# ScalarE's order in the attention phase of a fused attention, experts, scan and ternary FFN kernel

## What is computed

```
x = x + conv0(layernorm_c(x))   # e1, e2 = relu(w1 xn), relu(w2 xn); softmax(e1^T e2) mixes xn; + relu(w3 xn)
t = t + moe(layernorm(t))       # 16 experts, top 4 of each token, and a shared expert
x = x + scan(layernorm_c(x))    # rows top to bottom and back: relu(Wm carry + b) + row
t = t + ternary_ffn(layernorm(t))  # weights w / mean|w| rounded to -1, 0, 1; silu(gate) * up; down
```

## Time and profile before

| what | value |
|---|---|
| median of 3 runs | 1029.52 us |
| lowest to highest | 1026.97 to 1030.14 us |
| profiled execution, its own time | 1030.67 us |
| its span | 1029.0 us |
| busy share PE / DVE / ACT / POOL | 91% / 63% / 52% / 14% |

### The profile page before, as it was taken

One profiled execution on the slowest core, in us unless ns is written; L12 is line 12 of the kernel. 1 busy time (PEld: TensorE's weight loads), 2 busy tenths in 40 slices (PEclk: granted clock), 3 DMA queues, 4 the chain that ended last, 5 costly groups with the idle time before them and its releaser, 6 DMA issues. The chain is left out here.

```text
span 1029.0 us, 21177 instructions
## 1 busy us (share of the span) xinstructions
PE 939.9 (91%) x7748; PEld 617.7 (60%) x7749; DVE 651.2 (63%) x1272; ACT 538.3 (52%) x857; POOL 139.3 (14%) x165
## 2 busy tenths in 40 slices
PE   5988997899999999999999999999999949975796
PEld 4444544567766766766676677667754438862453
DVE  5366788456665645665656665665656776667773
ACT  3665596256564544564546655555653212234674
POOL 0000001102210110210120112012106800002000
PEclk9988998999999999999999999999999979997998
DMA  8770544776786576675568856867886510000001
GB/s 285 250 245 1 207 160 152 222 224 212 269 262 205 195 232 196 225 270 189 193 233 258 256 203 228 258 194 234 266 253 196 169 36 1 1 0 1 1 21 62
DMA packets 164882, 181.76 MB, mean 177 GB/s; under 512 B 54609, under 2 KB 132433, under 8 KB 164850
## 3 DMA queue, kind: packets, MB, share of 16 engines
q1 hardware_dynamic: 152338, 147.35, 44.4%
q0 software_dynamic: 9808, 32.12, 9.7%
q10 hardware_dynamic: 2704, 1.87, 0.6%
HBM read 155.09 MB, written 14.68 MB: 165 GB/s over the span
## 5 line engine op out<-in xcount | busy, mean ns | idle before, releaser
L1090 DVE SCALAR_TENSOR_TENSOR w_lo<-raw_first,w_hi 128x1024 f16<-128x1024 f32 x144 | 172.6, 1223 | 76.7 <-ACT w_hi L581 76.7
L848 PE MATMUL pa<-x,w_hi 128*128 128x256 f16 (+2 forms) x576 | 171.2, 297 | 8.3 <-DVE between L1097 5.7
L850 PE MATMUL pa<-x,w_lo 128*128 128x256 f16 (+2 forms) x576 | 171.1, 297 | 0.0
L849 PE MATMUL pa<-x,w_hi 128*128 128x256 f16 (+2 forms) x576 | 171.0, 297 | 0.0
L848 PE MATMUL pb<-x,w_hi 128*128 128x256 f16 (+2 forms) x576 | 170.9, 297 | 0.0
L849 PE MATMUL pb<-x,w_hi 128*128 128x256 f16 (+2 forms) x576 | 170.9, 297 | 0.0
L850 PE MATMUL pb<-x,w_lo 128*128 128x256 f16 (+2 forms) x576 | 170.8, 296 | 0.0
L581 ACT ACTIVATE w_hi<-raw_first 128x1024 f16<-128x1024 f32 x144 | 147.8, 1049 | 2.2 <-DMA raw_first<-in_gate_up 2.2
L589 ACT CAST early<-between 128x320 f16<-128x320 f32 (+1 forms) x144 | 68.4, 475 | 151.1 <-DVE between L1097 151.1
L1090 DVE SCALAR_TENSOR_TENSOR w_lo<-raw_last,w_hi 128x1024 f16<-128x1024 f32 x72 | 88.2, 1224 | 76.1 <-ACT w_hi L581 76.1
L1102 DVE TENSOR_TENSOR early<-between,early 128x320 f16<-128x320 f32 (+1 forms) x144 | 74.0, 514 | 74.2 <-ACT early L589 74.1
(11 more groups left out here) (273 smaller groups left out, 1623.0 us busy)
## 6 DMA issues: line engine op xcount, KB each, us to landing
raw_first<-in_gate_up SPq DMA_DIRECT2D x96, 512.0 KB, 4.7
raw_last<-in_gate_up SPq DMA_DIRECT2D x32, 512.0 KB, 3.9
raw_first<-in_down SPq DMA_DIRECT2D x32, 512.0 KB, 4.6
raw_last<-in_down SPq DMA_DIRECT2D x32, 512.0 KB, 3.6
chunks<-in_f SPq DMA_DIRECT2D x16, 704.0 KB, 5.7
slot_y<-chunks POOLq DMA_DIRECT2D x16, 512.0 KB, 3.2
chunks<-in_f SPq DMA_DIRECT2D x6, 768.0 KB, 4.8
raw_first<-in_sgate SPq DMA_DIRECT2D x6, 512.0 KB, 6.3
```

The source lines that it names most:

```text
L848: T.matmul(out, hi_a, hi_b, start=first, stop=False, **flags)
L849: T.matmul(out, hi_a, lo_b, start=False, stop=False, **flags)
L850: return T.matmul(out, lo_a, hi_b, start=False, stop=last, **flags)
L1090: V.scalar_tensor_tensor(w_lo[:, j % RING, c], raw[j % RING][:, c], W_SCALE, w_hi[:, j % RING, c], ALU.mult, ALU.subtract).then_inc(split_ ...
```

## The change

On ACT: behind `exp(3)`, `exp(4)`, `exp(5)` and `exp(6)` the next `relu` and `turned_copy` stand at once, ahead of the `hi`, `sum_abs` and `make_ternary` calls that preceded them. The scan's weight copy goes from ahead of `exp(3)` to behind `sum_abs(5)`. At `exp(7)`, `turned_copy(6)` changes places with `make_ternary(1)`. On DVE: the scan weights' four instructions go from behind `row_max(3)` to behind `row_max(5)` and `lo(0, 0, 1)`, and the two instructions of the ternary scale go from behind `add_attention(4)` to directly behind `row_max(6)`. PE, POOL and SP keep their lists. No instruction is added or removed.

```diff
 # ACT
             turned_copy(1)
+
+            exp(3)
+            relu(2)
+            turned_copy(2)
+            hi(0, 0, 0)
+            sum_abs(5)
             act.wait_ge(conv_in, 32)
             S.copy(conv_hi[:, :, :], conv).then_inc(conv_hi_ready, 1)
             S.copy(bias_hi[:, :], bias).then_inc(conv_hi_ready, 1)
-
-            exp(3)
-            hi(0, 0, 0)
-            sum_abs(5)
             sum_abs(6)
-            relu(2)
-            turned_copy(2)
             sum_abs(7)
 
             exp(4)
+            turned_copy(3)
             hi(0, 0, 1)
             sum_abs(8)
             sum_abs(9)
-            turned_copy(3)
             sum_abs(10)
 
             exp(5)
+            relu(3)
+            turned_copy(4)
             sum_abs(11)
             hi(0, 1, 0)
-            relu(3)
-            turned_copy(4)
             hi(0, 1, 1)
 
             exp(6)
-            make_ternary(0)
             turned_copy(5)
             hi(0, 2, 0)
+            make_ternary(0)
 
             exp(7)
             zn_copy(0)
             x_high(0)
+            turned_copy(6)
             make_ternary(1)
-            turned_copy(6)
             zn_copy(1)
             x_high(1)
 # DVE: these lines go from behind row_max(3) to behind lo(0, 0, 1)
             dve.wait_ge(conv_hi_ready, 2)
             link(V.tensor_tensor(conv, conv, conv_hi[:, :, :], ALU.subtract))
             link(V.tensor_tensor(bias, bias, bias_hi[:, :], ALU.subtract))
             step(V.tensor_scalar(conv_lo[:, :, :], conv, LOW_SCALE, None, ALU.mult))
             step(V.tensor_scalar(bias_lo[:, :], bias, LOW_SCALE, None, ALU.mult))
 # DVE
             row_max(6)
+            dve.wait_ge(abs_summed, 1)
+            link(V.tensor_scalar(inv_ws[:, :], abs_all[:, :], 1.0 / (C * W1), QEPS, ALU.mult, ALU.max))
+            V.reciprocal(w_scale[:, :], inv_ws[:, :]).then_inc(scale_ready, 1)
             make_tokens(FIRST)
             add_assembly(5)
             add_attention(4)
-            dve.wait_ge(abs_summed, 1)
-            link(V.tensor_scalar(inv_ws[:, :], abs_all[:, :], 1.0 / (C * W1), QEPS, ALU.mult, ALU.max))
-            V.reciprocal(w_scale[:, :], inv_ws[:, :]).then_inc(scale_ready, 1)
 
             row_max(7)
```

More of the change, by code:

```diff
@@ L1245, in _ @@
             row_max(3)
[L1246 to L1250, removed]
             add_assembly(2)
@@ L1260, in _ @@
             lo(0, 0, 1)
+            dve.wait_ge(conv_hi_ready, 2)
+            link(V.tensor_tensor(conv, conv, conv_hi[:, :, :], ALU.subtract))
+            link(V.tensor_tensor(bias, bias, bias_hi[:, :], ALU.subtract))
+            step(V.tensor_scalar(conv_lo[:, :, :], conv, LOW_SCALE, None, ALU.mult))
+            step(V.tensor_scalar(bias_lo[:, :], bias, LOW_SCALE, None, ALU.mult))
             add_assembly(4)
```

## The result

The changed kernel's median is 1018.87 us (4 runs, 1016.47 to 1020.67), against 1029.83 for the kernel before beside it (4 runs, 1026.97 to 1034.4). The ratio is 0.9883, with a 95% interval of 0.9856 to 0.9911: 9 to 15 us faster, 12.0 in the middle. Repeated later with more runs, the same kernel gave 0.9908 (0.9879 to 0.9936).

The account below looks back on a forecast made before the run. PE's two holes ended by ACT, ahead of the first `gate_up`, were taken as the bound. The schedule's 10.2 us less 1.7 for the clock gave 8.5 us, so a median of 1021.0 us, range 1018 to 1025.

Parts of the forecast that it names:

- What bounds the kernel: Phase ahead of the first `gate_up` at 103.36 us: PE has two long holes ended by ACT; the expert loop gives nothing.
- both holes: On PE: 4.25 us ahead of 54.37, `score(4)` waiting for `relu(2)`; 5.00 us ahead of 87.63, `turn_prob(6)` waiting for `turned_copy(5)`.
- The schedule: New lists on ACT, DVE and PE up to `turn_zn(1)`, which starts at 81.25 instead of 91.49: 10.2 us gained.
- The move of `turned_copy(6)`: ACT, ahead of `make_ternary(1)`: costs nothing, covered by `assemble(7)` and `route(0)`; without that cover up to 2.9 us.
- The chunk loads: Chunks 9 and 10 asked for later, with their `sum_abs` ahead of `exp(5)`: cost taken as nothing, bounds 0 and 6 us.
- the clock term: TensorE's clock falls behind the 2.5-us hole ahead of `turn_zn(1)`: 1.7 us lost, bounds 0 and twice 1.7.
- the row of a like wait: PE stood still 2.49 us up to 186.6, then was granted 0.59 over 3.4 us and 0.92 over 4: 1.7 us lost.
- no clock loss: Rival: TensorE's clock does not fall behind the hole ahead of `turn_zn(1)`; gain 10.2 us, 1019.3 us; chance 0.2.
- The late partition sum: Rival: POOL's sum stalls DVE behind `row_max(6)` by up to 7.4 us; gain 1.1 to 8.5, 1025 us; chance 0.08.
- the late chunk loads: Rival: `exp(5)` and the abs sums up to 6 us late; gain 2.5 to 7.5, say 1024.5 us; chance 0.08.
- swallowed behind the phase: Rival: something behind 103.36, such as weight loads on SP, has its own time; within 3 us of before, 1028; chance 0.07.
- The slower case: Rival: chunk loads held beyond the whole gain; gain gone at a 14.4-us landing, 1034 us at 19; chance 0.03.

Follow-up runs that it names:

- its two parts: Kernel before with only the first place changed (`exp(3)` to `exp(5)` order, scan weights): ratio 0.9934; with only the second (order behind `exp(6)`, `exp(7)`, ternary scale): 0.9956.
- the second place alone: Kernel before with only ACT's order behind `exp(6)` and `exp(7)` and the ternary scale's place on DVE changed: ratio 0.9956, 4.5 us.
- the early scale: Changed kernel with the ternary scale's two instructions directly behind DVE's sum of the abs parts: `turn_zn(1)` 38.2 us behind `row_max(3)` instead of 37.6.
- the scan weights in the idle places: Changed kernel with scan-weight copies directly behind `exp(3)` on ACT and their four DVE instructions behind `add_assembly(2)`: ratio 0.9899.

## Why the prediction was right or wrong

**What bounds the kernel** was right, and both holes went for the reasons given.

**The schedule** was right in each step that a row can check: `exp(4)` behind the whole ACT chain and PE waiting for it (1.42 us, forecast 1.2), DVE's list without a hole (20.05 us against 20.1), `turn_zn(1)` waiting for `x_low(0)` (2.34 against 2.5), the sum 10.2 us (measured 10.18, and 5.7 + 4.5 by its two parts). `turn_zn(1)` at 79.13 looks earlier than the forecast's 81.25, but the whole phase stands 2.18 us earlier in this profile: 79.13 + 2.18 = 81.31. The move of `turned_copy(6)`, costed at nothing, cost nothing: from `turn_zn(1)` to the first `gate_up` it is 11.82 us, and was 11.87. The chunk loads made ACT wait 1.2 us ahead of `sum_abs(10)`, for a load that took 6.0 us, and PE 0.39 us, without reaching DVE's list:

```profile
60.96 1.48 ACT L540 ACTIVATE rows<-chunks 128x1536 bf16<-128x1536 f32 x1 [1.21 <-DMA chunks<-in_f]
```

**The step that failed is the clock term.** The forecast took 1.7 us of loss as certain ("I take 1.7, as the row of a like wait shows it") and gave its absence a chance of 0.2. The size is about right where it fell: 13.5 and 13.2 us from `turn_zn(1)` to the first `gate_up` instead of 11.8, so 1.7 and 1.4. But behind holes of 2.2 to 2.7 us ahead of `turn_zn(1)` it fell in two of seven profiles (the second place alone, the early scale) and in none of four of the changed kernel, where the term measured nothing. By these profiles its likeliest value was nothing, and the likeliest total 10.2 us, which is 1019.3 us, the rival named "no clock loss". The row of the like wait was a poor guide. A wait of 2.4 to 3.0 us stands there, at the start of the expert loop, in all thirteen profiles, and the clock fell behind it in twelve, the four of the changed kernel among them. As long a wait ahead of `turn_zn(1)` was not followed by the same clock; why is open. The Trainium skill's rule that the forecast cites ("TensorE: Matmul & The Clock Gate", section "What's actually happening"), that the cold stretch varies from run to run of one kernel, agrees with the low clock early in the phase, present in two of four profiles of the changed kernel; ahead of `turn_zn(1)` those four agree with each other. The page says it of the cold matmuls at a kernel's start.

**The range was too narrow at its lower end.** It left 1.3 us below 1019.3 for the scatter. Of the 3.5 us between the forecast's 1021.0 and the 1017.5, 1.7 is the clock term. The other 1.8 is scatter, and that the first ratio fell on this side is chance: the repeat's 0.9908 makes 1020.0 of the 1029.52, inside the range. The scatter has places. The low clock early in the phase cost the first profile of before 1.7 us; PE's waits at the start of the expert loop differ by up to 4.3 us between profiles. Single runs of the kernel before lay between 1026.80 and 1035.91 us, those of the changed one between 1016.47 and 1024.54. What is left of 12.0 over 10.2 is within this scatter: the repeat gave 9.5, and the intervals of both hold 10.2.

**The rivals.** The late partition sum and the late chunk loads did not happen. Nothing was swallowed behind the phase. The slower case stayed away: the longest chunk load took 10.9 us in the changed kernel's first profile and 12.2 in the worst of its four, and none reached 14.

## What to carry to other kernels

With hand-ordered queues and one buffer between stages, put what another engine waits for directly behind what it depends on, and let the side work fill the time behind it; but then look at what the side work itself waits for, since one waiting instruction (here `make_ternary(0)` for the scale) blocks everything queued behind it. A new schedule can be worked out from start-to-start steps of the old trace, here to 0.1 us in 10.2, when each list is followed to the next wait; where the waits that come up behind a removed one were left out, as with the scan weights in the idle places, the sum was 1.5 us off. What such a sum does not give is the scatter of the clock and the loads around it, so a term that depends on the clock's state belongs in the range with a chance, not in the middle, and one wait of the same length at another place is no measure of that chance.

## What was not expected of the hardware

TensorE's clock behind short waits is not the same from profile to profile of one kernel. Behind two short waits of PE at 21 to 25 us it was low in two of the four profiles of the changed kernel and high in the other two. In the first and the third the two waits are the same to 0.01 us. First profile (the clock stayed high), then third (it fell):

```profile
22.74 0.70 PE L785 MATMUL ps<-early 64*128 64x256 f32 x2 [1.12 <-ACT early L519]
24.64 0.67 PE L785 MATMUL ps<-early 64*128 64x256 f32 x2 [1.20 <-ACT early L526]
```

```profile
22.69 0.70 PE L785 MATMUL ps<-early 64*128 64x256 f32 x2 [1.12 <-ACT early L519]
24.59 0.67 PE L785 MATMUL ps<-early 64*128 64x256 f32 x2 [1.21 <-ACT early L526]
```

Behind a single hole of 2.68 us it stayed at 2.4 GHz (third profile of the changed kernel), and behind one of 2.41 us it fell to 1.2 GHz (second place alone). At the start of the expert loop, where all thirteen profiles have a wait of 2.36 to 3.04 us, it fell in twelve; the thirteenth, that of the early scale, was granted 1.00 behind 2.52 us. The changed kernel's first profile there:

```profile
173.67 0.45 PE L848 MATMUL pa<-x,w_hi 128*128 128x320 f16 x1 [2.61 <-DMA x<-early]
```

```profile
173.67:177.07 3.40, 3.40 (x14) 1.98 (x15) 0.00 (x0) 0.72 (x1) 2.02 (x4) 0.54 1.03 353
```

So neither the length of a wait nor the kernel decides it alone; what differs between the places was not tested. And GpSimd's sum over 128 partitions of three columns is nearly as short as its row says: 0.60 us of waiting on DVE for a row of 0.43 us.
